# A fused attention and mixture-of-experts block: fp32 row-tiled scores, packed weights, GpSimd masks and column-tiled projections

## What is computed

```python
xn = layernorm(x)
# branch 1: one attention over 128 dims, then its own layernorm
q, k, v = split(xn @ w_qkv.T);  y = softmax(q @ k.T / sqrt(128)) summed over keys ... @ w_fc.T + b_fc
a1 = layernorm(xn + y) * gamma + beta          # einsum 'bqk,bvd->bqd': k and v are summed apart
# branch 2: 16 heads of 8 dims, causal, then four experts
h = rms(xn) * n1_w;  q, k = rms per head of (h @ wq.T), (h @ wk.T);  v = h @ wv.T
ao = softmax(causal(q @ k.T * 8**-0.5)) @ v @ wo.T;  ao[:, :, :32] = 0;  x1 = xn + ao
xf = rms(x1) * n2_w;  wts = top-2 of softmax(xf @ gate_w.T), normalised
o0 = gelu(xf @ e0_up.T) @ e0_down.T
o1 = silu(xf @ e1_w1.T) * (xf @ e1_w2.T) @ e1_down.T
o2 = gelu(gelu(gelu(xf @ l1.T) @ l2.T) @ l3.T) @ l4.T
o3 = gelu(gelu(xf @ e3_down.T) @ e3_up.T) @ e3_out.T
moe = sum_e wts[e] * o_e;  moe[:, :, :32] = 0
out = x + a1 + (x1 + moe)
```

## Time and profile before

| | |
|---|---|
| Time of the runs | 312.24 us median of 3 (310.26 to 313.15) |
| The profiled execution | span 316.5 us; no other time of it is given |
| Busy | PE 263.2, weight loads 203.3, DVE 174.5, ACT 154.0, POOL 82.3 us |
| PE instructions | 1861 matmuls, as many weight loads |
| DMA | 10.25 MB, mean 32 GB/s |
| Chain that ended last | PE 45%, "issue" 35%, ACT 8%, DVE 5%, POOL 4% |

### The profile page before, as it was taken

The page is one execution under the profiler, slowest core; times in us unless marked ns, Lnnn a source line. Parts: engine busy times, 40 slices in busy tenths (PEclk is TensorE's granted clock), DMA queues, the critical chain, the costliest instruction groups (busy, mean ns, idle before and its releaser), DMA issues.

```text
span 316.5 us, 5532 instructions
## 1 busy us (share of the span) xinstructions
PE 263.2 (83%) x1861; PEld 203.3 (64%) x1861; DVE 174.5 (55%) x732; ACT 154.0 (49%) x323; POOL 82.3 (26%) x161
## 2 busy tenths in 40 slices
PE   1546698589897989799979998998989898998694
PEld 0235275447686768676767776776776688677474
DVE  2095049515953696269724983389338746543603
ACT  1215255225644755465554655466537645643530
POOL 4964003510352025301540055004530033014000
PEclk9999559956999999999998999999999999999879
DMA  3900400210003100310030103010301021100000
GB/s 86 265 5 0 99 3 0 57 46 0 2 1 68 50 0 2 69 43 10 0 66 2 51 2 66 2 51 0 69 0 36 0 44 28 33 0 0 20 0 17
DMA packets 12856, 10.25 MB, mean 32 GB/s; under 512 B 1812, under 2 KB 11800, under 8 KB 12824
## 3 DMA queue, kind: packets, MB, share of 16 engines
q1 hardware_dynamic: 11816, 9.64, 12.2%
q10 hardware_dynamic: 1008, 0.21, 0.3%
HBM read 4.60 MB, written 1.05 MB: 18 GB/s over the span
## 4 chain that ended last, share of the span: by engine, by line
PE 45%; issue 35%; ACT 8%; DVE 5%; POOL 4%; DMA 1%; DVEq 0%; POOLq 0%; ACTq 0%
PE even_ps L1433 9%; PE down_ps L1459 5%; PE a_ps L1194 5%; PE a_ps L1286 5%; PE b_ps L1194 3%; PE even_ps L1422 3%; PE odd_ps L1442 2%; PE pv_ps L1345 2%; PE pv_ps L1459 2%; PE odd_ps L1422 2%; ACT x_sq L576 2%; ACT qkv L511 1%; PE scores_ps L1320 1%; ACT qT L553 1%; POOL k_lane L292 1%
## 5 line engine op out<-in xcount | busy, mean ns | idle before, releaser
L477 ACT ACTIVATE probs<-scores_ps 128x512 f32<-128x512 f32 x96 | 56.0, 598 | 33.5 <-PE scores_ps L1329 32.1
L396 POOL TENSOR_SCALAR ln_tmp<-ln_mv 128x2 f32<-128x2 f32 x8 | 4.8, 595 | 124.6 <-DVE ln_mv L1031 119.8
L1320 PE MATMUL scores_ps<-qT,k_lane 128*128 128x256 f32 x128 | 35.4, 368 | 0.5
L1329 PE MATMUL scores_ps<-later_keys,ident_bf 128*128 128x256 bf16 (+1 forms) x96 | 32.1, 335 | 0.0
L547 ACT ACTIVATE l_h<-even_ps 128x512 f32<-128x512 f32 x24 | 14.4, 598 | 31.0 <-PE even_ps L1433 25.7
L1320 PEld LDWEIGHTS scores_ps<-qT,k_lane 128*128 128x128 f32 x128 | 23.4, 208 | 7.5 <-issue 3.2
L1345 PE MATMUL pv_ps<-probs,v_aug 128*32 128x256 f32 x256 | 20.4, 390 | 6.2 <-DVE pvT L796 3.7
L1325 PE MATMUL scores_ps<-qT,k_lane 128*128 128x128 f32 x128 | 22.1, 297 | 3.8 <-ACT probs L477 3.8
L1058 DVE SCALAR_TENSOR_TENSOR acc<-down_ps,wts,acc 128x96 f32<-128x96 f32 x32 | 10.2, 318 | 27.1 <-issue 15.2
L1286 PE MATMUL a_ps<-qkvT,xnT 128*128 128x384 f32 x32 | 18.9, 682 | 6.1 <-ACT xnT L495 4.5
L1194 PE MATMUL a_ps<-ident,qk_parts 128*128 128x128 f32 x128 | 20.1, 280 | 4.5 <-ACT kT L561 1.6
(11 more groups left out here) (207 smaller groups left out, 635.3 us busy)
## 6 DMA issues: line engine op xcount, KB each, us to landing
k_lane<-kT SPq DMA_DIRECT2D x32, 128.0 KB, 2.4
x_sb<-in_L_attn_x SPq DMA_DIRECT2D x8, 128.0 KB, 2.4
acc<-in_L_attn_x SPq DMA_DIRECT2D x8, 128.0 KB, 2.2
out<-acc SPq DMA_DIRECT2D x8, 128.0 KB, 1.9
nat_l<-in_L_ffn_e_l SPq DMA_DIRECT2D x2, 256.0 KB, 4.6
nat_l<-in_L_ffn_e_l SPq DMA_DIRECT2D x2, 128.0 KB, 3.9
nat_qkv<-in_L_attn_w_qkv SPq DMA_DIRECT2D x1, 192.0 KB, 6.4
nat_e1a<-in_L_ffn_e_w SPq DMA_DIRECT2D x1, 128.0 KB
```

Of the source, the lines that this page charges most:

```text
L477: nc.scalar.activation(dst, src, ACT.Exp).then_inc(s["exp_done"], 1)
L1320: T.matmul(ps[:, i * SEQ:(i + 1) * SEQ], k_lane[p][:, 2 * part + i, g, 0:P], qT[p][:, g, :], start=i == 0, stop=False)
L1329: T.matmul(own, ident_bf[:], later_keys[:].unsqueeze(1).to_broadcast([P, blocks, P]), start=False, stop=True).then_inc(s["scores_full"], 1)
```

## The change

The kernel is rewritten around the same arithmetic. What it does:

- **Packed weights.** The host lays the weights out turned and side by side in five arrays; SP loads them with five DMAs, in rows of 1.5 to 5 KB. The transposes of weights, their copies and the zeroing of `k_lane` and `qk_parts` are gone. n2_w is applied when xfT is copied (`xf_copy`).
- **Scores.** q and k stay fp32. `qk_turn` has 4 transposes. ACT copies kT four times, once for each group, with a scale per row that is zero outside the 8 rows of the group's head (`k_copy`). `scores(n, g)` is called four times a batch: 8 calls in four row tiles of 32, 4 of 256 and 4 of 128 columns, each lane into its own PSUM bank. The four banks are one buffer, so the next group waits for both exponentials of this one. There is no mask matmul and no DMA to `k_lane`.
- **Exponentials and masks.** ACT has 8 exponentials a batch, of 128x768. Behind each, POOL sets the masked places to 0 with an affine_select of 128x512 (`mask`), and `weigh_v` waits for that.
- **Block turns.** DVE's transpose of 32x32 blocks takes the place of the copy of pv (`pv_turn`) and of the second turn (`ao_turn`); PE's `pv_turn` and `ao_turn` and ACT's `ao_copy` are gone.
- **Column tiles of 64.** `down`, `wo_project` and `gate` make each call twice, for 64 tokens each.
- **Own lag per operation.** There are twelve slots; each operation names the batch it works on by its own distance (0 to 4). The lists are in another order; PSUM banks and their fills are redistributed (bank a, pv, even, odd). ACT's list now goes from exponentials to GELUs and back twice in a slot.

The core of the diff:

```diff
+BANK_FILLS = {
+    "a": (("QKV1", 1), ("Q0T", 1), ("S00", 2), ("S01", 2), ("FC", 2), ("QKT", 1), ("XT", 0), ("QKV0", 0)),
+    "pv": (("PV0", 2), ("XFT", 3), ("GATE", 3), ("PV1", 2), ("PV2", 2), ("PV3", 2), ("WO", 2)),
+    "even": (("DN0", 4), ("E1A", 3), ("L1", 3), ("L2", 3), ("L3", 3)),
+    "odd": (("DN1", 4), ("E1B", 3), ("E0", 3), ("D3", 3), ("U3", 3)),
+}
...
-            for name, src in (("e1a", e1_w1), ("e1b", e1_w2), ("l1", e2_l1), ("e0u", e0_up), ("e3u", e3_up)):
-                sp.dma_start(nat_up[name][:], src.rearrange("(c p) d -> p c d", p=P)).then_inc(s["w_up_in"], 16)
...
+            sp.dma_start(proj[:], w_proj).then_inc(s["proj_in"], 16)
+            sp.dma_start(first[:], w_first).then_inc(s["first_in"], 16)
...
+            def mask(n, u):
+                pool.wait_ge(s["exp_done"], UNITS * n + u + 1)
+                nc.gpsimd.affine_select(out=own, in_=own, compare_op=ALU.is_ge, fill=0.0, base=0,
+                                        pattern=[[0, 2 * TILES], [1, P]], channel_multiplier=-1
+                                        ).then_inc(s["masked"], 1)
...
+                wait(act, "scores_full", GROUPS * n + g + 1)
+                fill_ready(act, f"PV{(g - 2) % GROUPS}", n if g >= 2 else n - 1)
+                nc.scalar.activation(probs[g % 2][:, 2 * half:2 * half + 2, 0:SEQ + P],
+                                     scores_ps[:, 2 * half:2 * half + 2, 0:SEQ + P], ACT.Exp).then_inc(s["exp_done"], 1)
...
+                ins = nc.scalar.activation(kT[n % 2][:, g, :], ps_of("QKT")[:, SEQ:2 * SEQ], ACT.Copy,
+                                           scale=k_rows[:, g:g + 1])
...
+                V.transpose(pv_rows[:, g].rearrange("p n e -> p (n e)"), ps_of(f"PV{g}")[:, 0:SEQ]
+                            ).then_inc(read_sem(f"PV{g}"), 1)
...
-                            T.matmul(ps[:, i * SEQ:(i + 1) * SEQ], k_lane[p][:, 2 * part + i, g, 0:P], qT[p][:, g, :],
-                                     start=i == 0, stop=False)
...
-                    T.matmul(own, ident_bf[:], later_keys[:].unsqueeze(1).to_broadcast([P, blocks, P]), start=False,
-                             stop=True).then_inc(s["scores_full"], 1)
+                wait(pe, "exp_done", UNITS * n + HALVES * g)
+                for kt in range(TILES):
+                    for lane in range(LANES):
+                        rows = slice(32 * lane, 32 * lane + 32)
+                        ps = scores_ps[:, lane, 0:SEQ] if kt == 0 else scores_ps[:, lane, SEQ:SEQ + P]
+                        ins = T.matmul(ps, kT[p][rows, g, kt * P:(kt + 1) * P], qT[p][rows, kt * P:SEQ],
+                                       start=kt == 0, stop=kt == 1 and not searching, tile_position=(32 * lane, 0))
...
-                            ins = T.matmul(ps[:, e * KEPT:(e + 1) * KEPT], hidden[e][:, ci, j * P:(j + 1) * P],
-                                           downT[e][:, ci * P + MASKED:(ci + 1) * P], start=(ci == 0), stop=(ci == HC - 1))
+                        for rows in COLUMN_TILES:
+                            tokens = slice(j * P + rows.start, j * P + rows.stop)
+                            ins = T.matmul(ps_of(fill)[rows, e * KEPT:(e + 1) * KEPT], hidden[e][:, ci, tokens],
+                                           downs[:, e, ci, MASKED:], start=(ci == 0), stop=(ci == HC - 1),
+                                           tile_position=(0, rows.start))
```

More of the change, by code:

```diff
@@ new lines, in fused_block, with live @@
+        s = {n: sem(n) for n in names + [f"{bank}_{what}" for bank in banks for what in ("full", "read")]}
+        x_in, acc_in, out_done = ([sem(f"{n}{p}") for p in range(2)] for n in ("x_in", "acc_in", "out_done"))
+        SLOTS = BATCHES + SLOTS_AFTER
+        at = fill_ordinals(BATCHES, SLOTS)
+        ROUND_LIST = [(j, kt) for j in range(TILES) for kt in range(j + 1)]
+        ROUNDS = len(ROUND_LIST)
+        block = ctx.enter_context(nc.Block())
+        def live(n):
+            return 0 <= n < BATCHES
@@ L623, in _ @@
+            x_copy(0)
+            act.wait_ge(s["m0_full"], 1)
+            nc.scalar.activation(m0[:], scores_ps[:, 0, 0:D], ACT.Copy, scale=float(D) ** -0.5).then_inc(s["m0_ready"], 1)
+            act.wait_ge(s["vfc_full"], 1)
+            nc.scalar.copy(vfc[:], scores_ps[:, 1, 0:D]).then_inc(s["vfc_ready"], 1)
+            ahead = 1
+            for t in range(SLOTS):
+                slot(t)
         @block.vector
@@ L1190, in _ @@
             T = nc.tensor
+            searching = False
+            ahead = 0
             def turn(dst, src):
@@ new lines, in qkv_project, with qk_turn @@
+            def qkv_project(n, j):
+                if not ahead <= n < BATCHES:
+                    return
+                fill = f"QKV{j}"
+                fill_free(pe, fill, n)
+                fill_emptied(pe, "XT", n)
+                if n == 0:
+                    pe.wait_ge(s["proj_scaled"], 1)
+                T.matmul(ps_of(fill)[:, 0:3 * D], xnT[n % 2][:, j * P:(j + 1) * P], qkvT[:], start=True, stop=True
+                         ).then_inc(full_sem(fill), 1)
+            def qk_turn(n):
+                if not live(n):
+                    return
+                fill_free(pe, "QKT", n)
+                wait(pe, "qk_ready", n + 1)
+                for part in range(2):
+                    for j in range(TILES):
+                        heads = qk_n[:, j, part * HEADS:(part + 1) * HEADS, :].rearrange("p h e -> p (h e)")
+                        at_col = part * SEQ + j * P
+                        ins = turn(ps_of("QKT")[:, at_col:at_col + P], heads)
+                ins.then_inc(full_sem("QKT"), 1)
@@ new lines, in wo_project @@
+            def wo_project(n):
+                if not live(n):
+                    return
+                fill_free(pe, "WO", n)
+                wait(pe, "ao_ready", n + 1)
+                for j in range(TILES):
+                    for rows in COLUMN_TILES:
+                        tokens = slice(j * P + rows.start, j * P + rows.stop)
+                        ins = T.matmul(ps_of("WO")[rows, j * P:j * P + KEPT], aoT[:, tokens], woT[:, MASKED:], start=True,
+                                       stop=True, tile_position=(0, rows.start))
+                ins.then_inc(full_sem("WO"), 1)
@@ new lines, in slot @@
+            def slot(t):
+                qkv_project(t - 1, 1)
+                scores(t - 2, 1)
+                weigh_v(t - 2, 0)
+                q0_project(t - 1)
+                down(t - 4, 0)
+                down(t - 4, 1)
+                a0_scores(t - 2, 0)
+                xf_turn(t - 3)
+                scores(t - 2, 2)
+                gate(t - 3)
+                up_layer(t - 3, "E1A", e1T[:, 0:HID])
+                a0_scores(t - 2, 1)
+                weigh_v(t - 2, 1)
+                scores(t - 2, 3)
+                up_layer(t - 3, "E1B", e1T[:, HID:])
+                fc_row(t - 2)
+                weigh_v(t - 2, 2)
+                up_layer(t - 3, "L1", l1T)
+                up_layer(t - 3, "E0", e0uT)
+                qk_turn(t - 1)
+                square_layer(t - 3, "L2", l2T, l1_h, "L1")
+                up_layer(t - 3, "D3", e3dT)
+                weigh_v(t - 2, 3)
+                x_turn(t)
+                find_maxima(t - 1)
+                scores(t - 1, 0)
+                qkv_project(t, 0)
+                square_layer(t - 3, "L3", l3T, l2_h, "L2")
+                e3_up_layer(t - 3)
+                wo_project(t - 2)
```

2226 lines of the change are left out of this document (1041 added, 1185 removed).

## The result

The changed kernel takes 232.36 us (median of 4 runs, 231.04 to 233.08). The kernel before, run beside it on the same chip, takes 312.69 (4 runs, 310.26 to 313.31). The ratio is 0.745, with a 95% interval of 0.739 to 0.751. The forecast was 246 us with a range of 228 to 268: the direction and the range held, and the time was 14 us too high. The profiled execution has a span of 231.3 us, where the sum forecast 249.

The account below looks back on a forecast made before the run. PE's list was taken to set the slot: 23.75 us of work plus 3.0 of waits made 26.7. Savings over all stretches took the span from 316.5 to 249 us, and factor 0.987 gave 246 us, range 228 to 268.

Parts of the forecast that it names:

- What bounds the kernel: Full slots, between ACT's copies of qT: PE's list sets their length, with PE busy for 29.2 of 32.5 us.
- PE's work: Full slot: 29.2 us less scores 2.9, turns 2.4, column tiles 0.6, plus 0.45 for tiling changes, gives 23.75 us.
- Change of tiling: PE going in and out of tiled calls costs 0.14 to 0.33 us; three new places add 0.45 a slot.
- I keep 3.0: PE's waits in a full slot, 3.3 us before, were put at 3.0, giving a slot of 26.7 us.
- the waits nearly vanish: Rival, chance 0.14: waits of 1.5 us a slot, start 22, slot two 15; 231 us.
- The rival in which ACT's ring sets the slot: Chance 0.14: scores, exponentials, masks and table switches set the slot; 29.5 us a slot, 262 us in all.
- POOL and masks: Full slot: eight affine_selects at 0.6 us add 4.8, POOL at 13.4 us, below PE's 23.75, so free as work.
- Weight loads beside each other: New tiles: loads overlap, a down takes 1.6 us; the rival, chance 0.08, had them not overlap, about 270 us.
- The slow rival: Chance 0.04: tiles run one after another, a group of scores takes 2.6 us; 328 us, slower than before.
- Start: Start to the first qT copy: 33.4 us before, 24 forecast, as late weights, zeroing and successive fills go.
- End: Stretch behind the last qT copy: 54.6 us before, 46.5 forecast, with shorter downs and fewer waits for the gate.

Follow-up runs that it names:

- e3_whole_rows: Scores without row tiles, each call taking all 128 rows, against the changed kernel: 283.79 us, ratio 0.914 to the kernel before.
- e6_no_cover: Changed kernel with scores(t-1, 0) put behind qkv_project(t, 0), so nothing stands between x_turn and the call needing its copy: 242.21 us, ratio 0.777 to the kernel before.
- e7_two_loads: Changed kernel with ACT's first two exponentials moved behind the GELUs of L3 and U3, two table loads fewer a slot: 279.41 us, ratio 0.897 to the kernel before.
- e4_no_mask: Changed kernel with POOL's masks left out, weigh_v waiting for the exponentials alone: 229.29 us, ratio 0.737 to the kernel before.
- b1_packed: Kernel before with packed weights alone, the zeroing of k_lane kept: 321.27 us, beside 321.98 for the kernel before in that group.
- f1_logits_early: Changed kernel with the output projection in whole tiles and DVE's copy of the logits four operations earlier in its list: 232.11 us.

## Why the prediction was right, and where it was wrong

- **What bounds the kernel: right.** PE's list sets the slot, before and after. In the full slots PE's row is empty for 0.12 us.
- **PE's work: right, 23.75 forecast and 23.70 measured; that it is this close is partly luck.** Scores: 3.6 forecast, 4 x 0.86 = 3.44 measured, and 0.47 more in the calls beside them by e3_whole_rows, so 0.3 too low. Two downs: 3.2 forecast, 2.79 measured. Output projection and gate: 0.3 gained together forecast, 0.06 measured. Change of tiling at the three new places: 0.45 forecast; in the calls beside them 0.18 at the downs and 0.17 at the projection are measured, nothing at the gate, whose neighbour ahead is tiled too. These misses, +0.3, -0.4, +0.2 and -0.1, cancel. The turns were priced at 0.11 each, and the four that are left take 0.44; no run put the others back.
- **The step that failed: "I keep 3.0" of waits in a slot.** Measured were 0.12 in PE's row, and some 0.2 more that the row hides, ahead of weigh_v(t-2, 1). The 3.0 was carried over as a sum, because the order was new and ACT busier. The trace of before had it in four waits, which the prediction should have looked up one by one. They are, in PE's timeline's slot: 1.13 us for the copy of qT, 0.56 for xnT, 0.77 for an exponential and 0.73 ahead of the last weigh_v, 3.2 together. The profile puts the last one down to the copy of pvT, but that copy had ended 0.75 us before:

```profile
149.69 1.23 ACT L477 ACTIVATE probs<-scores_ps 128x512 f32<-128x512 f32 x2 [0.97 <-PE scores_ps L1329]
149.86 0.42 DVE L796 COPY pvT<-pv_ps 128x256 f32<-128x256 f32 x1
151.03 0.64 PE L1345 MATMUL pv_ps<-probs,v_aug 128*32 128x256 f32 x8 [0.73 <-DVE pvT L796]
```

  What ended at 150.92, just ahead of weigh_v, are the group's last two exponentials, for which it waits as well. For each of the four the new list says what becomes of it. qk_turn has one fill, and L2, D3 and weigh_v stand between it and x_turn. scores(t-1, 0) stands between x_turn and what needs it, and e6_no_cover put just that wait back. A group's weigh_v no longer follows its scores at once: for the last group five layers of experts, a weigh_v and more stand between. Groups of scores are spaced by 2.8 to 7.7 us of other calls, and e7_two_loads shows the price when the exponentials are late. That the waits for qT and for the last exponentials are covered is read from the list and from their absence in the trace; these were not put back.
- **What this step explains of the 17.7 us.** The five full slots, four and the one without a load, came out 13.7 shorter than forecast, nearly all of it by this step. Slot three is 4.6 shorter for another reason: it was priced as a full slot, but PE is busy for only 18.25 us in it, 5.5 less than the 23.75, and idle for 3.9, 0.9 more than the 3.0. The start (-3.3) and the end (+3.8) cancel.
- **The rival "the waits nearly vanish", 231 us, came nearest, in part by luck.** Its waits of 1.5 were 0.12 and its start of 22 was 20.7, but slot two is 19.05 for its 15, and the end is 3.8 longer than it has. That the forecast's own 19 for slot two was met to 0.05 is luck as well, as the same slot takes 16.66 to 19.05 in three traces.
- **ACT: right.** 20.4 forecast, 20.36 measured; exponentials 809 ns for 0.82 us; four table loads a slot at 1.28. The rival in which ACT's ring sets the slot did not happen, but it was near: e7_two_loads is that rival by one move in ACT's list, and it costs 47 us, part of it by the clock. What decides is the position of the exponentials in the list, not their sum, which that kernel made smaller.
- **DVE: wrong by 3.1 us a slot, without consequence.** 16.5 forecast, 19.59 measured. The prediction named the likely cause (POOL beside DVE) and priced it at nothing in DVE's own busy time. Nine Newton steps and two short steps (L742, L930) take 2.6 us longer than the same steps in the slot of before. The masks alone are 0.9 of it, 18.69 in a full slot without them; the other POOL operations were not taken away. The block turn was right: 439 ns for the copy's 420.
- **POOL and masks: right within 3 us.** 13.4 forecast, 13.2 measured, 635 ns a mask for 600. "Cost nothing" is at most 3.4 us by e4_no_mask, 1.4 of it in the full slots and slot three.
- **Weight loads beside each other: right, the rival fell.** 32 loads and 32 matmuls of a down take 1.37 us, less than the 16 and 16 of a whole one (1.76 in the earlier trace rows), and PE's and PEld's rows run beside each other all through it. This speaks against the rule of the Trainium skill, TensorE: Matmul & The Clock Gate, The mechanism, that a load overlaps only beside a matmul of another row group: here the tiles differ in columns alone. The measurement decides.
- **The slow rival: wrong in its premise, right in its price.** Tiles one after another would be 2.61 a group, as e3_whole_rows measures. Even so that kernel is faster than the one before, 0.914, since the rest of the change stands.
- **Start: right size, wrong reason in part.** 24 forecast, 20.7 measured. The prediction listed weights, zeroing and fills together. b1_packed shows that the weights alone bring no gain; by the rows the memset beside DVE, the splits and the four fills are the gain.
- **End: wrong by 3.8 us.** 46.5 forecast behind the last mark, 50.3 measured. `down` is now four slots behind the load, not three, so a larger part of PE's work lies behind the last qT copy: 42.9 of 202.3 us, before 45.4 of 263.2. PE is idle there for 7.4 of the 50.3 us, up to 0.78 us ahead of single calls, because the other batches that covered them are done.

## What to carry to other kernels

Look up each wait of the engine that sets the time, by name, and decide for each what the new order does with it; a sum of waits carried over says nothing about the new order. Compare the named releaser's end with the end of the wait: where it had long ended, look for another that ended just then. A wait that is moved away can come back at the next bank, as in f1_logits_early. Where an engine is full, a call of 0.9 us placed between a turn and its reader is worth more than a call made a tenth faster, and in a ring of engines a table load is cheaper than a late producer. Weights, zeroing and copies ahead of a first batch count only if they lie on the chain that ends last there; take them away one at a time in thought, and see what is late next.
